# Diagonal score maxima by bank: several heads' narrow units share one PSUM bank, one mask product and one VectorE reduction

## The reference

```
h = token_table_sum(x)                          # four context tables, gathered and added
h = h + attention(layernorm(h))                 # 32 query heads, 8 key heads, head size 32
h = h + ffn(layernorm(h))                       # one 1024 x 1024 product; low-rank part in a Fourier basis
scores = q @ k.T / sqrt(32); scores = where(causal, scores, -1e20)
attn = softmax(scores);      out = attn @ v
```

## Time and profile before

| what | value |
|---|---|
| median of three runs | 3563.59 us (3561.82 to 3579.18) |
| profiled execution, device time | 3567.09 us |
| its span | 3565.3 us |
| mean granted TensorE clock | 0.978 of 2.4 GHz |
| part B's 16 groups | 751.7 to 2797 us of the span |
| masks of the maxima (L982) | 1024 instructions |
| reductions (L918) | 2560 instructions |

### The profile page before, as it was taken

One profiled execution on the slowest core, in us unless ns is written; L12 is line 12 of the kernel. 1 busy time (PEld: TensorE's weight loads), 2 busy tenths in 40 slices (PEclk: granted clock), 3 DMA queues, 4 the chain that ended last, 5 costly groups with the idle time before them and its releaser, 6 DMA issues. The chain is left out here.

```text
span 3565.3 us, 61290 instructions
## 1 busy us (share of the span) xinstructions
PE 3413.7 (96%) x25088; PEld 2362.2 (66%) x25088; DVE 2288.3 (64%) x3914; ACT 1421.9 (40%) x1677; POOL 2266.6 (64%) x1042
## 2 busy tenths in 40 slices
PE   1999999999999999999999999999999799999999
PEld 1778888646666566566566666666665488888887
DVE  3677777667777777777777777777775344444443
ACT  2222232135555555555555555555555301111010
POOL 4443220159889889889989989998998622222221
PEclk8999999979999999999999999999999899999999
DMA  8999874721221122122122122112212234333332
GB/s 230 248 255 233 238 207 132 208 77 33 57 62 49 43 64 57 36 62 56 38 68 60 28 61 59 45 42 62 50 39 63 83 88 94 93 90 90 94 95 65
DMA packets 248219, 334.59 MB, mean 94 GB/s; under 512 B 64346, under 2 KB 153818, under 8 KB 247938
## 3 DMA queue, kind: packets, MB, share of 16 engines
q1 hardware_dynamic: 229506, 263.54, 27.3%
q0 software_dynamic: 18432, 67.12, 8.8%
HBM read 227.80 MB, written 101.71 MB: 92 GB/s over the span
## 5 line engine op out<-in xcount | busy, mean ns | idle before, releaser
L918 DVE TENSOR_REDUCE mpart<-mx_ps 128x1 f32<-128x512 f32 (+3 forms) x2560 | 1429.6, 604 | 530.1 <-PE mx_ps L982 342.6
L876 ACT ACTIVATE probs<-st_ps 128x1024 f32<-128x1024 f32 (+1 forms) x1152 | 1063.9, 974 | 828.2 <-PE st_ps L1017 642.7
L979 PE MATMUL mx_ps<-k_max,qs 96*128 96x512 f32 (+3 forms) x2560 | 907.5, 415 | 16.3 <-DVE mpart L918 12.3
L1017 PE MATMUL st_ps<-qs,k_score 98*128 98x512 f32 (+1 forms) x2304 | 719.9, 407 | 0.2
L850 POOL TENSOR_TENSOR sums<-probs 128x1024 f32<-128x1024 f32 x256 | 610.1, 2383 | 160.4 <-ACT probs L876 160.4
L979 PEld LDWEIGHTS mx_ps<-k_max,qs 96*128 96x128 f32 x2560 | 463.9, 194 | 313.1 <-DVE mpart L918 206.1
L852 POOL TENSOR_TENSOR sums<-sums,probs 128x1024 f32<-128x1024 f32 x256 | 609.7, 2381 | 37.8 <-ACT probs L876 19.9
L1035 PE MATMUL od_ps<-probs,vs 128*32 128x256 f32 (+1 forms) x9216 | 595.3, 376 | 0.0
L858 POOL TENSOR_TENSOR sums<-sums,probs 128x1024 f32<-128x1024 f32 (+1 forms) x256 | 543.8, 2124 | 20.3 <-ACT probs L876 0.3
L1017 PEld LDWEIGHTS st_ps<-qs,k_score 98*128 98x128 f32 x2304 | 421.3, 194 | 72.6 <-ACT probs L876 12.3
L1210 POOL TENSOR_TENSOR h<-h,bb 128x1024 f32<-128x1024 f32 x32 | 104.1, 3254 | 509.1 <-DVE xn_c L1284 509.1
(11 more groups left out here) (108 smaller groups left out, 4076.5 us busy)
## 6 DMA issues: line engine op xcount, KB each, us to landing
qs<-q_hi_scratch SPq DMA_DIRECT2D x128, 256.0 KB, 4.8
h_scratch<-hbuf SPq DMA_DIRECT2D x32, 512.0 KB, 8.3
q_hi_scratch<-rot_hi SPq DMA_DIRECT2D x64, 256.0 KB, 4.0
q_lo_scratch<-rot_lo SPq DMA_DIRECT2D x64, 256.0 KB, 4.7
qs<-q_lo_scratch SPq DMA_DIRECT2D x64, 256.0 KB, 5.8
o_scratch<-od_sb SPq DMA_DIRECT2D x128, 128.0 KB
o_in<-o_scratch SPq DMA_DIRECT2D x32, 512.0 KB, 5.0
o_in<-recip_scratch SPq DMA_DIRECT2D x128, 128.0 KB, 8.1
```

The costliest lines, as they stand in the source:

```text
L876: nc.scalar.activation(probs[:, n % SLOTS, half, :, lo:QW], st_ps[:, half, :, lo:QW], ACT.Exp, scale=float(HD) ** -0.5).then_inc(exp_done, 1)
L918: nc.vector.tensor_reduce(mpart[:, h * TPC + t, kc:kc + 1], mx_ps[:, e % MAX_BANKS, 0:w], AX, ALU.max).then_inc(max_done, 1)
L979: mm = nc.tensor.matmul(out, qs[c][0:K_ROWS, h, t * P:(t + 1) * P], k_max[0:K_ROWS, kc * CT:kc * CT + w], start=True, stop=not diagonal)
L1017: mm = nc.tensor.matmul(out[:, :, lo:QW], k_score[0:M_ROW + 2, kt * P:(kt + 1) * P], qs[c // 2][0:M_ROW + 2, h:h + 2, at + lo:at + QW], st ...
```

## The change

On the diagonal, the units of tile 0 (128 columns) of all four heads become one unit, and the units of tile 1 (256 columns) become one for two heads each. Tiles 2 and 3 and everything off the diagonal stay one head a unit. A unit's heads lie side by side in one bank. Each head has its own score product (only the first with the start flag, which clears the bank's accumulation state); one mask product with the mask repeated along the columns (a broadcast moving operand) serves all; one reduction gives one result a head. A group then has 140 units in place of 160 (44 diagonal), 144 entries in place of 164, and their placing on the steps follows from the same formula.

```
 def max_units():
-    return [(c, kc, t, h) for c in range(QC) for kc in range(c + 1) for t in range(TPC) for h in range(GROUP)]
+    heads_of = lambda diagonal, t: GROUP // (t + 1) if diagonal and t < 2 else 1
+    return [(c, kc, t, range(h, h + heads_of(kc == c, t))) for c in range(QC) for kc in range(c + 1)
+            for t in range(TPC) for h in range(0, GROUP, heads_of(kc == c, t))]
...
             def row_max(g, n, unit):
-                c, kc, t, h = MAXES[unit]
+                c, kc, t, heads = MAXES[unit]
                 e, w = g * NE + n, CT if kc < c else (t + 1) * P
+                rows = slice(heads[0] * TPC + t, heads[-1] * TPC + t + 1, TPC)
+                scored = mx_ps[:, e % MAX_BANKS, 0:len(heads) * w].rearrange("p (h w) -> p h w", w=w)
...
-                nc.vector.tensor_reduce(mpart[:, h * TPC + t, kc:kc + 1], mx_ps[:, e % MAX_BANKS, 0:w], AX, ALU.max
-                                        ).then_inc(max_done, 1)
+                nc.vector.tensor_reduce(mpart[:, rows, kc], scored, AX, ALU.max).then_inc(max_done, 1)
...
             def row_scores(g, e, unit):
-                c, kc, t, h = MAXES[unit]
-                if t == 0 and h == 0 and kc == 0:
+                c, kc, t, heads = MAXES[unit]
+                if t == 0 and heads[0] == 0 and kc == 0:
                     pe.wait_ge(q_loaded[c], LOAD * (g + 1))
-                if t == 0 and h == 0 and kc == c:
+                if t == 0 and heads[0] == 0 and kc == c:
                     pe.wait_ge(k_max_loaded[c], LOAD * (g + 1))
                 diagonal = kc == c
-                w = (t + 1) * P if diagonal else CT
-                out = mx_ps[:, e % MAX_BANKS, 0:w]
-                mm = nc.tensor.matmul(out, qs[c][0:K_ROWS, h, t * P:(t + 1) * P],
-                                      k_max[0:K_ROWS, kc * CT:kc * CT + w], start=True, stop=not diagonal)
+                w, many = (t + 1) * P if diagonal else CT, len(heads)
+                out = mx_ps[:, e % MAX_BANKS, 0:many * w].rearrange("p (h w) -> p h w", w=w)
+                for j, h in enumerate(heads):
+                    mm = nc.tensor.matmul(out[:, j], qs[c][0:K_ROWS, h, t * P:(t + 1) * P],
+                                          k_max[0:K_ROWS, kc * CT:kc * CT + w], start=j == 0, stop=not diagonal)
                 if diagonal:
-                    mm = nc.tensor.matmul(out[:, w - P:w], ident_m, mqk, start=False, stop=True)
+                    over = mqk.rearrange("p (h w) -> p h w", h=1).broadcast_to([P, many, P])
+                    mm = nc.tensor.matmul(out[:, :, w - P:w], ident_m, over, start=False, stop=True)
                 mm.then_inc(max_ready, 1)
```

## The result

The changed kernel takes 3503.21 us (median of 4 runs, 3501.15 to 3505.48), the kernel before on the same chip 3562.70 (3559.94 to 3579.18): ratio 0.9821, 95% interval 0.9806 to 0.9837. The profiled execution took 3505.48 us around a span of 3503.7. One execution of a later experiment (the paired masks with early queries) took 5030.18 us at a mean granted clock of 0.653 and is in no comparison.

The account below looks back on a forecast made before the run. The prediction took PE's own time in part B as the bound. Gains of 19.7 (PE work), 5 (subtractions) and 2 us (group 0), less 0.5 for loads, made 26 us: 3538 us forecast, range 3524 to 3557.

Parts of the forecast that it names:

- DVE's long subtractions: Groups 2 to 9: PE stalls behind the 2.4 us L946; 0.6 us a group saved, 5 us, between 0 and 15.
- Of PE's work only weight loads wait, under a running product: Undisturbed groups: only weight loads wait for DVE, 0.4 us at the longest, hidden under a running product; no gain counted.
- DVE's shorter list is worth nothing by itself: Part B: reductions fall from 11.3 to 8.2 us a group, but PE hides both, so no gain.
- Masks, surcharges, back-to-back queries: PE, each group: masks gain 0.41 us, surcharges 1.46, back-to-back query products lose 0.60; 1.23 us net with 0.04 more lost.
- Start: Group 0: every third step holds eight entries, not nine, saving reductions in four such steps, 2 us.
- Order of loads: Group transitions: last query chunk needed one step earlier, its loads just in time; price 0.5 us over 15 transitions.
- The queries came late: Rival, second entry of step 2: each transition waits and runs at low clock, 45 us lost against 26, 3583 us; chance 0.04.
- Exposed weights: Rival, back-to-back query products: each load costs 0.19 us, not 0.11, 15 us less gain, 3553 us; chance 0.08.
- a mask cut up: Rival, wide masks: the program splits them one piece a head, keeping 64 masks a group, 3552 us; chance 0.03.
- slow broken outputs: Rival, two-head masks: the gap between column runs doubles their 0.125 us, giving back 16 us, 3554 us; chance 0.03.
- the stalls stay whole: Rival, groups 2 to 9 keep their 3.8 us and group 0 its waits: 19 us gained, 3545 us; chance 0.12.

Follow-up runs that it names:

- paired masks with early queries: Changed kernel with adjacent diagonal units' products before both masks, and next group's chunk 3 queries issued ahead of a value load: 3487.13 to 3495.68 us, ratio 0.9800.
- the 128-column units alone: Kernel before with only tile 0's four-head units joined, tile 1 left at one head a unit: 3544.62 us, ratio 0.9930.
- the run with halved reductions: Kernel before with each DVE reduction over the first half of its columns, PE's work unchanged: 3515.38 us in one run, against 3567.15.
- the run with one column: Kernel before with the L946 subtraction on 1 column instead of 512, ScalarE copying the rest: 3553.33 us in one run, against 3567.15.

## Why the prediction was too small

**"DVE's long subtractions"** is the step that failed: 5 us, between 0 and 15, and 26.3 were measured. I read 2.4 us as the length of L946 and asked only how PE gets over it. The length alone is 0.68 us; the rest was a wait behind a POOL addition, which DVE's records count as busy. The trace before would have shown it: instructions of one form take from 2416 to 2769 ns for 512 columns, where a reduction of 512 columns takes 683, and POOL's rows beside them end 0.55 us before they do. Its bounds failed with it, for I capped the gain at half of 8 x 3.8 us, and even the 3.8 held for six of the eight groups only (27.1 us in all, some 9 of them the low clock). These 26 us are real, but that all of them came is luck: nobody chose where the subtraction falls, one number moved gave 25 of them without the change, and with the change other places for it left 21.6 us of stall. How much the sparser list would give with the subtraction held as long at steps 12 and 14 is open; the 10 us of the 128-column units alone say that it need not be nothing.

**"Of PE's work only weight loads wait, under a running product"** was wrong by 0.91 us a group, 14.6 us in all: a term put at nothing. I took the longest wait (0.4 us) as hidden without subtracting ends there. "DVE's shorter list is worth nothing by itself" held: the run with one reduction a head shows it. Its price didn't: the list got 1.4 us a group shorter (22.3 over 16 groups), not 3.1.

**Masks, surcharges, back-to-back queries**, 1.23 us a group or 19.7 in all, held: 1.26 us a group by the run with halved reductions, and the costs one by one, 0.22 to 0.23 for the wide mask, 0.111 for the product behind its like, no surcharge behind wide masks. This is the part that reading ends instead of busy time gave.

**Start**: 2 us gain forecast, 1.4 us loss measured. The clock stood at 0.50 for 17.0 us from group 0's start and for 3.4 us later; before, it was for 8.8 us:

```profile
751.70:760.50 8.80, 8.80 (x27) 4.91 (x25) 5.81 (x10) 3.25 (x4) 1.27 (x1) 0.50 0.01 4
```

At the 1.5 us that 3.4 us of low clock cost in a disturbed group, the 11.6 us more would cost some 5, which leaves group 0 some 3.7 us shorter without them (an estimate; 2 + 1.23 were forecast). Over all profiled kernels group 0 took 129 to 141 us, so this term can't be judged here. **Order of loads**: right in place, with 0.8 us or more in hand in most groups. The changed kernel waited for queries in group 4 (0.08 us) and group 7 (0.20 us), and the 0.8 us that groups 2 to 9 take above the rest stands against the 0.5 taken as price.

**The rivals.** None held. The queries came late twice and briefly, as just said. Exposed weights, a mask cut up and slow broken outputs would each show in the ends above and don't; the Trainium skill's rule that non-contiguous patterns slow matmuls significantly (PSUM — Partial Sum Buffer, Specifications (TRN2)) is not borne out at 0.13 us for 256 columns in two runs. That the stalls stay whole was the rival I gave most to, for the same reason as the step that failed: it hung on "its length", which wasn't one. In the kernels with half of the change, and in the changed kernel with the subtractions moved, they do stay in part.

**Open.** Why the clock stays low longer in group 0, and why just this spacing brings DVE to the subtraction 0.2 us ahead of an addition's end, were not tried. POOL's additions were not taken away; that they hold the subtraction rests on ends that agree to 0.02 us, on the run with one column and on the moves. Why the product behind a narrow mask pays more was not tested either; that the next weights load is not covered stays a reading of the prediction. Nor was the placing of the units changed by itself, to show what took away the 0.91 us of waits and the low clock.

## What to carry to other kernels

An instruction that is much longer than others of its width may be waiting inside its own record, as the subtraction was here. Look at what GpSimd runs at that moment before reckoning with its length, and try another place for it: one number was worth 25 us here. A PE that is busy throughout at full clock can still hide waits, here of 0.10 to 0.25 us; subtract ends at the steps where most work arrives. In this kernel the short bf16 masks among float32r products were cheapest wide or next to each other.

## What was new about the hardware

- A DVE subtraction of two SBUF operands (512 columns) ended 0.55 to 0.56 us behind the GpSimd addition (128x1024, 2.38 us) that ran when DVE reached it, and with a single column 0.02 behind. GpSimd's next addition then took 2.7 us behind the 512 columns and 2.35 to 2.37 behind the single one.
- Reductions of 512 columns from PSUM cost nearly the same with one result or four. Groups by form of the changed kernel:

```profile
L922 DVE TENSOR_REDUCE mpart<-mx_ps 128x1 f32<-128x512 f32 x1792 | 1154.8, 685 | 364.8 <-PE mx_ps L983 237.0 <-PE mx_ps L987 97.5 <-DVE mcol L925 0.5
L922 DVE TENSOR_REDUCE mpart<-mx_ps 128x2 f32<-128x512 f32 x128 | 85.2, 687 | 42.2 <-PE mx_ps L987 42.2
L922 DVE TENSOR_REDUCE mpart<-mx_ps 128x4 f32<-128x512 f32 x64 | 44.3, 693 | 41.3 <-PE mx_ps L987 41.3
```

- A float32r product behind a 128-column bf16 mask paid 0.053 to 0.058 us more here, behind two such masks once, and behind 256 or 512 columns nothing (0.232 to 0.233 us for 512 columns, against 0.285 to 0.289 behind the narrow mask).
